# Expert stage of a two-block Flamingo kernel: one row buffer and one result buffer for every tile, eight weight buffers, and an earlier gelu table load

## The chip, the core and the metric

The kernel runs on one core of one Trainium2 chip. The metric is the device time of one execution in microseconds (us); the time given for a kernel is the median of several runs. TensorE is called PE here, VectorE DVE, ScalarE ACT, GpSimd POOL and SyncE SP. An engine executes its own list of instructions in order and waits for others by semaphores. SP and ACT also issue DMAs; a DMA raises a semaphore by 16 when it has landed.

## What is computed

The input is x (4 batches of 256 tokens, 128 features) and a context of 512 rows of 96 features for each batch. Four residual blocks follow one another: single-head cross-attention with softmax, a feed-forward block whose operands are quantized to FP4 and back, 16-head cross-attention with a small feed-forward tail, and a mixture of 8 experts, of which every token takes one. All are preceded by a layer norm and multiplied by a tanh gate. The part that the change touches is the last block:

```python
router_probs = jax.nn.softmax(x @ Wr, axis=-1)
expert_idx = jnp.argmax(router_probs, axis=-1)
p_max = jnp.max(router_probs, axis=-1, keepdims=True)
def expert_mlp(w1, bb1, w2, bb2):                  # 128 -> 512 -> 128
    h = jax.nn.gelu(x @ w1 + bb1, approximate=False)
    return h @ w2 + bb2
outs = jax.vmap(expert_mlp)(W1, b1, W2, b2)        # 8 experts
out = p_max * jnp.einsum('te,etd->td', onehot, outs)
...
x = x + jnp.tanh(g_ffn[1]) * out
```

## The kernel before

Up to about 281 us of the span the kernel works through the first three blocks and the routing, batch by batch, in an order written out by hand (CHAINS, walked by `walk` on every engine). At the end of each batch, POOL scatters that batch's 256 finished rows to `row_dram`, a buffer in DRAM with one region for each expert. Such a row of 260 numbers (PAY) holds the normed input of the expert (128), the residual (128), the gate, and the token's number. Each scatter raises `rows_scattered`.

Then comes the expert stage. 1024 tokens in tiles of 128 rows, where a tile belongs to one expert, are at most 8 + 7 = 15 tiles (TILES). DVE works out a plan from the counts (14 small steps, semaphore `plan_dve`): for each tile its expert and the DRAM row at which it begins, both put into `exp_i`. Unused tiles point to blank rows, whose token number lies out of range, so that nothing is written for them; they go through the same work.

For tile k each engine has one share:

- **SP** (`load_rows`) reads the tile's DRAM row out of `exp_i` into a register (`row_of`, a TENSOR_LOAD and two register steps, L436) and issues the load of 128 rows of 260 numbers from `row_dram` to `xg` (L439).
- **ACT** (`w1_load`, L1157 and L1158) reads the tile's expert in the same way and issues the load of that expert's first matrix (256 KB) to a slot of `w1s`. In `act_tile` it computes four gelus of 128x128 (L1166) and then issues a further `w1_load`.
- **PE** turns the rows (`pe_turn`, one transpose, L895), multiplies by the first matrix (`pe_up`, four products in two halves) and by the second (`pe_down`: a product that adds the bias, then four that each wait for one gelu). The second matrices of all experts stand in SBUF. The order in the loop is turn(k+2), up(k+1), down(k).
- **DVE** copies the turned rows from PSUM (`dve_turned`, L1555) and forms gate times result plus residual into `eo` (`dve_tile`, L1565).
- **POOL** scatters `eo` to the output by token number (L1875), one indirect DMA for each tile.

In the profile the names `xg`, `eo`, `xgT`, `ehT` all appear as `pT`, because these buffers are parts of that tensor, and many PE instructions have the line of a helper (L564).

Buffers go round in rings of RING = 5: `xg`, `eo`, `xgT`, `ehT` and `w1s`. The row load of tile k, from tile 5 on, therefore waits until the scatter of tile k-5 has landed (`out_scattered[k % 5]`, in `load_rows`), because that scatter reads the token numbers out of the same part of `xg`. The weight load of tile k+5 is issued after the gelus of tile k. `load_rows` reads the first five row numbers into registers, then waits for `rows_scattered`, then issues five loads.

Of the kernel before, what the change touches and what calls it, by code (L numbers as in the profile page):

```python
# [5 lines left out]
ALU = mybir.AluOpType  # L6
# [19 lines left out]
RING = 5  # L26
# [139 lines left out]
def flamingo_kernel(nc, a):  # L166
    out = a["out"]
    with ExitStack() as ctx:
# [45 lines left out]
        w1s = sb("w1s", [P, RING * F])  # L214
# [122 lines left out]
        xg = pT[:, 0:RING * PAY]  # L337
        o = RING * (PAY + D)
        xgT = pT[:, o:o + RING * P]
        ehT = pT[:, o + RING * P:o + RING * (P + F)]  # L340
        b1_pick = pT[:, o + RING * (P + F):o + RING * (P + F) + TILES * FC * E]
        eo = pT[:, RING * PAY:RING * (PAY + D)]
# [49 lines left out]
        rows_loaded = [sem(f"rows_loaded{u}") for u in range(RING)]  # L392
        out_scattered = [sem(f"out_scattered{u}") for u in range(RING)]
        e_turned, e_up, e_down = sem("e_turned"), sem("e_up"), sem("e_down")
        e_xT, e_act, e_out = sem("e_xT"), sem("e_act"), sem("e_out")
        w1_slot_loaded = [sem(f"w1_slot_loaded{u}") for u in range(RING)]
# [36 lines left out]
        def load_rows(sp):  # L433
# [4 lines left out]
            def load(k, row):  # L438
                sp.dma_start(xg[:, (k % RING) * PAY:(k % RING + 1) * PAY], row_dram[bass.ds(row, P), :]  # L439
                             ).then_inc(rows_loaded[k % RING], 16)  # L440
# [12 lines left out]
        def _(sp):  # L453
# [105 lines left out]
            for u in range(RING):  # L559
                sp.wait_ge(out_scattered[u], 16 * (TILES // RING))  # L560
# [307 lines left out]
        def slot(x, u, w):  # L868

            u = u % RING  # L870
            return x[:, u * w:(u + 1) * w]
# [18 lines left out]
        def pe_turn(pe, k):  # L890

            pe.wait_ge(rows_loaded[k % RING], 16 * (k // RING) + 16)
# [4 lines left out]
        def pe_up(pe, k):  # L897

            pe.wait_ge(e_xT, k + 1)
            pe.wait_ge(w1_slot_loaded[k % RING], 16 * (k // RING) + 16)  # L900
            if k >= 2:
                pe.wait_ge(e_act, FC * (k - 1))
            for half in range(2):
                for c in (2 * half, 2 * half + 1):
                    last = mm(up_bank(k, c), slot(w1s, k, F)[:, c * P:(c + 1) * P], slot(xgT, k, P))
                last.then_inc(e_up, 1)

        def pe_down(pe, k, e):
# [4 lines left out]
            for c in range(FC):  # L913
                pe.wait_ge(e_act, FC * k + c + 1)
                last = mm(down_bank(k), slot(ehT, k, F)[:, c * P:(c + 1) * P], w2e[:, bass.ds(e * F + c * D, D)], False,
# [984 lines left out]
```

## Time and profile before

| what | value |
|---|---|
| time, median of 3 runs | 345.93 us (345.71 to 347.42) |
| time of the profiled execution | 347.22 us |
| its span, first to last instruction | 345.5 us |
| PE busy | 262.1 us, 76% |
| DVE busy | 196.7 us, 57% |
| ACT busy | 159.7 us, 46% |
| POOL busy | 97.7 us, 28% |
| mean DMA rate | 89 GB/s |

The span is the time from the first to the last instruction of the profiled execution; 1.7 us of its time lie around the span. Busy shares are means over the whole program. The expert stage takes about the last 60 us of it, and what bounds that stage is read from windows, waits and the chain there. The expert tiles are slow or fast with the clock that TensorE was granted, 1.2 or 2.4 GHz, shown as 0.50 or 1.00 in the windows.

### The profile page before, as it was taken

The numbers are of one execution on the slowest core, as the hardware profiler recorded it, in microseconds if no ns is written. First come the engines' busy times: TensorE is split into PE (matmuls) and PEld (weight loads), VectorE is DVE, ScalarE is ACT, GpSimd is POOL, SyncE is SP. The second block draws the span as 40 slices with busy tenths as digits, with TensorE's granted clock in tenths as the row PEclk, the third lists the DMA queues.
The fourth block names the chain that finished last, engine by engine and source line by source line (L and its number), as shares of the span: only waits on it lengthen the run. The fifth ranks groups of instructions, "written<-read, shape, count | busy, mean of one in ns | idle before, by whom it ended". The sixth has DMA issues, their size and how long they took to land.

```text
span 345.5 us, 7087 instructions
## 1 busy us (share of the span) xinstructions
PE 262.1 (76%) x2617; PEld 144.2 (42%) x2617; DVE 196.7 (57%) x509; ACT 159.7 (46%) x371; POOL 97.7 (28%) x224
## 2 busy tenths in 40 slices
PE   3689477586877999979769998989976422968874
PEld 1236134132432435544335453444432212858764
DVE  6953775538993789797895767676521161111211
ACT  2335324453256548675544857366851202323331
POOL 5003314522462213451413412310320120132323
PEclk9999699769996999999988999699987555598999
DMA  4697792830052010232101321030000008254410
GB/s 112 197 264 250 258 308 85 265 108 9 2 161 77 6 37 4 73 100 72 38 1 41 61 82 38 31 73 1 3 33 0 0 15 244 71 150 109 148 42 8
DMA packets 30032, 30.89 MB, mean 89 GB/s; under 512 B 5445, under 2 KB 25116, under 8 KB 29998
## 3 DMA queue, kind: packets, MB, share of 16 engines
q1 hardware_dynamic: 18029, 16.06, 16.8%
q10 hardware_dynamic: 11104, 12.78, 11.7%
q0 software_dynamic: 864, 1.59, 1.4%
q8 instruction: 21, 0.34, 0.4%
q14 instruction: 14, 0.11, 0.1%
HBM read 15.28 MB, written 15.42 MB: 89 GB/s over the span
## 4 chain that ended last, share of the span: by engine, by line
PE 46%; DVE 25%; ACT 8%; DMA 7%; POOL 6%; issue 6%; SPq 1%; POOLq 0%; ACTq 0%; DVEq 0%
PE psC L564 10%; DVE nmx L1454 8%; PE psB L564 7%; PE psA L564 7%; PE psX L569 5%; PE psG L569 5%; PE psD L569 5%; DMA pT<-row_dram 3%; ACT pT L1119 3%; DMA out_rows<-pT 3%; POOL rstd L1669 2%; PE psG L564 1%; PE psD L575 1%; DMA qs<-nmT 1%; DVE stat L1227 1%
## 5 line engine op out<-in xcount | busy, mean ns | idle before, releaser
L1454 DVE TENSOR_REDUCE nmx<-psB 128x1 f32<-128x512 f32 x128 | 82.9, 680 | 28.3 <-PE psB L564 27.5
L1119 ACT ACTIVATE pT<-psA 128x512 f32<-128x512 f32 x128 | 72.0, 599 | 15.2 <-PE psA L564 13.8
L564 PE MATMUL psB<-ks,qs 112*128 112x512 bf16 x128 | 49.8, 402 | 8.5 <-DVE nmx L1454 8.0
L564 PE MATMUL psA<-qs,ks 115*128 115x256 bf16 x256 | 50.2, 282 | 6.2 <-ACT pT L1119 4.2
L564 PE MATMUL psC<-pT,v_live 128*32 128x256 f32 x512 | 37.0, 439 | 0.7 <-ACT pT L1119 0.7
L564 PEld LDWEIGHTS psA<-qs,ks 115*128 115x128 bf16 x256 | 20.2, 99 | 32.3 <-ACT pT L1119 12.9
L1875 POOL DMA_INDIRECT out_rows<-pT x15 | 14.8, 983 | 43.8 <-DVE pT L1565 43.5
L564 PEld LDWEIGHTS psB<-ks,qs 112*128 112x128 bf16 x128 | 12.5, 100 | 29.1 <-DVE nmx L1454 19.9
L564 PEld LDWEIGHTS psC<-pT,v_live 128*32 128x32 f32 x512 | 17.5, 126 | 16.9 <-issue 9.1
L569 PE MATMUL psG<-guT,xqT 128*32 128x352 f32 x128 | 15.1, 551 | 3.5 <-DVE u L1324 3.5
L1051 ACT ACTIVATE p<-psD,nmx 128x512 f32<-128x512 f32 x8 | 5.5, 688 | 26.6 <-DVE nmx L1303 26.6
L1166 ACT ACTIVATE pT<-psA,b_tiles 128x128 f32<-128x128 f32 x32 | 9.4, 367 | 17.1 <-PE psA L564 17.1
L1129 ACT COPY ou<-psC 128x256 f32<-128x256 f32 x16 | 5.9, 367 | 23.8 <-PE psC L564 23.8
L1679 POOL CAST nmp<-nmx 128x8 bf16<-128x8 f32 x16 | 3.1, 192 | 46.9 <-DVE nmx L1454 46.9
L569 PE MATMUL psD<-k0T,q0T 128*32 128x512 f32 x64 | 12.0, 833 | 3.8 <-DVE x_all L1317 3.2
L1819 POOL DMA_INDIRECT row_dram<-pay,desti x8 | 8.3, 1032 | 22.8 <-DVE count L1547 21.6
L1662 POOL TENSOR_TENSOR ve<-mv,eps_t 128x2 f32<-128x2 f32 x16 | 3.2, 199 | 38.7 <-DVE mv L1231 38.7
L1166 ACT ACTIVATE pT<-psB,b_tiles 128x128 f32<-128x128 f32 x28 | 8.1, 368 | 12.9 <-PE psB L564 12.9
L895 PE MATMUL psD<-ident,pT 128*128 128x128 f32 x8 | 2.8, 344 | 14.5 <-DMA pT<-row_dram 14.5
L1689 POOL TENSOR_TENSOR q_norm<-hid,q_inv 128x352 f32<-128x352 f32 x8 | 6.3, 788 | 25.2 <-DVE q_inv L1257 25.2
L1695 POOL TENSOR_TENSOR hid<-q_add,q_scale 128x352 f32<-128x352 f32 x8 | 6.3, 787 | 22.4 <-DVE q_add L1275 22.4
L1565 DVE SCALAR_TENSOR_TENSOR pT<-psC,pT 128x128 f32<-128x128 f32 x8 | 2.8, 351 | 16.8 <-PE psC L564 16.8
(227 smaller groups left out, 492.3 us busy)
## 6 DMA issues: line engine op xcount, KB each, us to landing
row_dram<-ou ACTq DMA_DIRECT2D x13, 650.0 KB, 6.2
w1s<-in_L_ffn_W ACTq DMA_DIRECT2D x15, 256.0 KB, 2.8
ks<-k_parts SPq DMA_DIRECT2D x16, 192.0 KB, 3.2
pT<-row_dram SPq DMA_DIRECT2D x15, 130.0 KB, 2.7
k_parts<-k1p SPq DMA_DIRECT2D x4, 384.0 KB, 3.2
qs<-q_parts SPq DMA_DIRECT2D x16, 96.0 KB, 3.5
k_parts<-k1p SPq DMA_DIRECT2D x4, 256.0 KB, 3.2
ctx_in<-in_ctx SPq DMA_DIRECT2D x4, 192.0 KB, 2.7
```

Source lines behind the costliest of these rows:

```text
L564: return nc.tensor.matmul(o, l, r, start=start, stop=stop, **k)
L569: last = nc.tensor.matmul(o[32 * j:32 * j + 32, :], l[:, 32 * j:32 * j + 32], r, start=start, stop=stop, skip_group_check=True)
L1051: nc.scalar.activation(p0[:, :], psD[:, :], ACT.Exp, bias=nmx0[:, t:t + 1], accum_out=sum0[:, t:t + 1]).then_inc(*aact.step(b, f"p{t}"))
L1119: nc.scalar.activation(pT[:, o:o + 512], psA[:, (i % 2) * 512:(i % 2) * 512 + 512], ACT.Exp).then_inc(*probs.step(b, f"e{g}_{i}"))
L1129: nc.scalar.copy(ou[:, g * LQ:(g + 1) * LQ], psC[:, 0:LQ]).then_inc(*ou_ready.step(b, f"g{g}"))
L1166: nc.scalar.activation(slot(ehT, k, F)[:, c * P:(c + 1) * P], up_bank(k, c), ACT.Gelu, bias=b1_tiles[:, k * FC + c:k * FC + c + 1]).then_i ...
L1454: nc.vector.tensor_reduce(nmx[:, col:col + 1], psB[:, (i % 2) * 512:(i % 2) * 512 + 512], AX_X, ALU.max, negate=True).then_inc(*maxima.ste ...
L1669: nc.gpsimd.tensor_tensor(rstd[:, o:o + NT], ve[:, o:o + NT], neg_half[:, :], ALU.pow).then_inc(*steps.step(b, f"{p}_rs"))
L1689: nc.gpsimd.tensor_tensor(q_norm[:, o:o + n].rearrange("p (n i) -> p n i", i=QB), src.rearrange("p (n i) -> p n i", i=QB), wide(q_inv[:, o ...
L1695: nc.gpsimd.tensor_tensor(dst.rearrange("p (n i) -> p n i", i=QB), q_add[:, o:o + n].rearrange("p (n i) -> p n i", i=QB), wide(q_scale[:, ...
L1819: nc.gpsimd.indirect_dma_start(row_dram[:, :], bass.IndirectOffsetOnAxis(desti[:, t:t + 1].bitcast(U32), 0), pay[:, t * PAY:(t + 1) * PAY] ...
L1875: nc.gpsimd.indirect_dma_start(out, bass.IndirectOffsetOnAxis(token, 0), eo[:, u * D:(u + 1) * D], None, bounds_check=T - 1, oob_is_err=Fa ...
```

## The change

Each of the 15 tiles gets its own part of `xg` and of `eo`. For this, `xgT` goes round in a ring of 3 and `ehT` in a ring of 2, and `b1_pick` moves from `pT` to `q_norm`. `load_rows` no longer waits for scatters: it reads a row number and issues that tile's load, fifteen times over, and waits for `rows_scattered` once, after the first row number. The weights get eight slots (W1_RING); ACT issues eight weight loads ahead of its first gelu, and the load of tile k+8 after the gelus of tile k. The throwaway gelu that makes ACT load the gelu table stands ahead of the wait for the plan and no longer behind the weight loads. DVE's wait for `out_scattered` in `dve_tile` goes, and the five `out_scattered` semaphores become one, which SP waits for at the end.

```diff
-RING = 5
+W1_RING = 8
+XT_RING = 3
+H_RING = 2
...
-        xg = pT[:, 0:RING * PAY]
...
-        eo = pT[:, RING * PAY:RING * (PAY + D)]
+        o = TILES * (PAY + D)
+        xg = pT[:, 0:TILES * PAY]
+        eo = pT[:, TILES * PAY:o]
+        xgT = pT[:, o:o + XT_RING * P]
+        ehT = pT[:, o + XT_RING * P:o + XT_RING * P + H_RING * F]
+        b1_pick = q_norm[:, 0:TILES * FC * E]
...
             sp.wait_ge(plan_dve, PLAN)
-            rows = {k: row_of(k) for k in range(RING)}
-            sp.wait_ge(rows_scattered, 16 * B * NT)
-            for k in range(RING):
-                load(k, rows[k])
-            for k in range(RING, TILES):
+            for k in range(TILES):
                 row = row_of(k)
-                sp.wait_ge(out_scattered[k % RING], 16 * (k // RING))
-                load(k, row)
+                if k == 0:
+                    sp.wait_ge(rows_scattered, 16 * B * NT)
+                sp.dma_start(xg[:, k * PAY:(k + 1) * PAY], row_dram[bass.ds(row, P), :]).then_inc(rows_loaded[k], 16)
...
-            if k + RING < TILES:
-                w1_load(act, k + RING)
+            if k + W1_RING < TILES:
+                w1_load(act, k + W1_RING)
...
+            nc.scalar.activation(th[:, 0:1], gains[:, 0:1], ACT.Gelu)
             act.wait_ge(plan_dve, PLAN)
-            for k in range(RING):
+            for k in range(W1_RING):
                 w1_load(act, k)
-            nc.scalar.activation(th[:, 0:1], gains[:, 0:1], ACT.Gelu)
...
-            if k >= RING:
-                dve.wait_ge(out_scattered[u], 16 * (k // RING))
```

On SP, at the start of the row loads, the order before was as follows. TENSOR_LOAD and "ISA x2" are one `row_of`; the single ISA is the register step of a load. Four more pairs of `row_of` rows stand where the dots are, then four more loads.

```order
L436 TENSOR_LOAD exp_i [waits plan_dve]
L436 ISA x2
...
L439 ISA [waits rows_scattered]
L439 DMA pT<-row_dram 128x260
...
L436 TENSOR_LOAD exp_i
L436 ISA x2
L439 ISA [waits out_scattered0]
L439 DMA pT<-row_dram 128x260
```

The same place with the change:

```order
L438 TENSOR_LOAD exp_i [waits plan_dve]
L438 ISA x2
L445 ISA [waits rows_scattered]
L445 DMA pT<-row_dram 128x260
L438 TENSOR_LOAD exp_i
L438 ISA x2
L445 ISA
L445 DMA pT<-row_dram 128x260
```

One row number instead of five now stands ahead of the first load, one more stands between any two loads, and no load waits for a scatter.

On ACT, between the last activation of the routing (lexp) and the first gelu of the experts, the order before was this, with four more weight loads where the dots are:

```order
L1151 ACTIVATE lexp<-lsub 128x16 [waits tail_dve]
L1157 TENSOR_LOAD exp_i [waits plan_dve]
L1157 ISA x2
L1158 ISA
L1158 DMA w1s<-in_L1_ffn_W1 128x512
...
L1217 ACT_TABLE_LOAD
L1217 ACTIVATE th<-gains 128x1
L1166 ACTIVATE pT<-psA,b1_tiles 128x128 [waits e_up,tile_bias_ready]
```

With the change, and seven more weight loads at the dots:

```order
L1146 ACTIVATE lexp<-lsub 128x16 [waits tail_dve]
L1208 ACT_TABLE_LOAD
L1208 ACTIVATE th<-gains 128x1
L1152 TENSOR_LOAD exp_i [waits plan_dve]
L1152 ISA x2
L1153 ISA
L1153 DMA w1s<-in_L1_ffn_W1 128x512
...
L1161 ACTIVATE pT<-psA,b1_tiles 128x128 [waits e_up,tile_bias_ready]
```

The table load moved ahead of the wait for the plan, and three more weight loads stand ahead of the first gelu.

## Rows read from the trace of the kernel before

**Rows 1.** Waits of PE from 286 us: engine tile line <- releaser: us, times, longest.
```profile
PE psD L895 <- DMA pT<-row_dram: 14.5, 4, 10.6
PE psX L895 <- DMA pT<-row_dram: 3.9, 3, 2.4
```

**Rows 2.** Waits of SP's queue from 280 us, same columns.
```profile
SPq L439 <- DMA out_rows<-pT: 32.2, 8, 11.4
```

**Rows 3.** Chain that ended last: start us, us, what.
```profile
303.10 3.50 DMA out_rows<-pT
306.76 3.00 DMA pT<-row_dram
```

**Rows 4.** PE's timeline: start us, us, line, op, out<-in [idle before <-releaser].
```profile
296.57 2.08 PE L564 MATMUL psC<-w2e,pT 128*128 x8
...
300.71 1.19 PE L564 MATMUL psG<-w2e,pT 128*128 x8
...
303.00 1.16 PE L564 MATMUL psC<-w2e,pT 128*128 x8
...
309.81 0.33 PE L895 MATMUL psD<-ident,pT 128*128 128x128 f32 x1 [2.51 <-DMA pT<-row_dram]
...
311.14 2.08 PE L564 MATMUL psC<-w2e,pT 128*128 x8
...
314.96 1.16 PE L564 MATMUL psG<-w2e,pT 128*128 x8
...
317.21 1.16 PE L564 MATMUL psC<-w2e,pT 128*128 x8
...
336.32 1.16 PE L564 MATMUL psC<-w2e,pT 128*128 x8
```

**Rows 5.** Windows: stretch, us, busy of PE PEld DVE ACT POOL, PEclk, DMA share, GB/s.
```profile
286.00:290.80 4.80, 0.00 (x0) 0.00 (x0) 0.15 (x1) 0.77 (x1) 0.00 (x0) 0.50 0.84 233
290.80:300.50 9.70, 9.13 (x37) 7.87 (x38) 1.34 (x5) 3.85 (x12) 0.66 (x1) 0.50 0.44 144
300.50:310.80 10.30, 7.12 (x55) 6.25 (x54) 1.83 (x6) 3.09 (x11) 3.29 (x4) 0.98 0.50 132
310.80:314.20 3.40, 3.40 (x18) 3.20 (x17) 0.55 (x2) 0.97 (x4) 0.00 (x0) 0.54 0.50 121
314.20:340.00 25.80, 21.25 (x160) 18.49 (x159) 4.92 (x16) 10.37 (x36) 8.84 (x9) 0.99 0.31 87
```

**Rows 6.** Line L436, 284 to 288 us: count, ns min/median/max, first and last start.
```profile
L436 SPq TENSOR_LOAD <-exp_i x5: 266/269/494, 284.5 to 287.0; - x5
...
L436 SPq SEQ_ASSERT  x5: 18/18/33, 285.2 to 287.5; - x5
```

**Rows 7.** Line L1819, the last two scatters to `row_dram`, same columns, then their landing.
```profile
L1819 POOL DMA_INDIRECT row_dram<-pay,desti x2: 963/1002/1042, 282.2 to 283.5; - x2
...
DMA to landing us min/median/max: 2.6/2.7/2.7
```

**Rows 8.** Line L439, the first five row loads, same columns, then their landing.
```profile
L439 SPq DMA_DIRECT2D pT<-row_dram x5: 332/333/398, 287.7 to 289.9; - x5
...
DMA to landing us min/median/max: 3.0/4.4/4.9
```

**Rows 9.** ACT's timeline (ACTq is its queue of DMA issues), columns as in rows 4.
```profile
285.39 4.62 ACTq L1158 DMA_DIRECT2D w1s<-in_L_ffn_W  x5
290.04 1.28 ACT L1217 ACT_TABLE_LOAD   x1 [10.03 <-issue]
...
293.00 0.63 ACT L1166 ACTIVATE pT<-psA,b_tiles 128x128 f32<-128x128 f32 x2 [1.47 <-PE psA L564]
...
316.71 1.14 ACT L1166 ACTIVATE pT<-psB,b_tiles 128x128 f32<-128x128 f32 x4 [1.18 <-PE psB L564]
```

**Rows 10.** POOL's timeline, the last two scatters of results.
```profile
340.80 0.98 POOL L1875 DMA_INDIRECT out_rows<-pT  x1 [1.16 <-DVE pT L1565]
342.08 0.98 POOL L1875 DMA_INDIRECT out_rows<-pT  x1 [0.30 <-issue]
```

More of the change, by code:

```diff
@@ L213, in flamingo_kernel @@
         wr = sb("wr", [P, E])
-        w1s = sb("w1s", [P, RING * F])
+        w1s = sb("w1s", [P, W1_RING * F])
         b1T = sb("b1T", [P, FC * E])
@@ L336, in flamingo_kernel @@
         exp_i = sb("exp_i", [P, 2 * TILES], I32)
-        xg = pT[:, 0:RING * PAY]
[L338 to L341, printed above, removed]
-        eo = pT[:, RING * PAY:RING * (PAY + D)]
+        o = TILES * (PAY + D)
[4 more added lines that the diff above has]
+        b1_pick = q_norm[:, 0:TILES * FC * E]
         tg = sb("tg", [P, 4])
@@ L391, in flamingo_kernel @@
         plan_dve = sem("plan_dve")
-        rows_loaded = [sem(f"rows_loaded{u}") for u in range(RING)]
-        out_scattered = [sem(f"out_scattered{u}") for u in range(RING)]
+        rows_loaded = [sem(f"rows_loaded{k}") for k in range(TILES)]
+        out_scattered = sem("out_scattered")
         e_turned, e_up, e_down = sem("e_turned"), sem("e_up"), sem("e_down")
         e_xT, e_act, e_out = sem("e_xT"), sem("e_act"), sem("e_out")
-        w1_slot_loaded = [sem(f"w1_slot_loaded{u}") for u in range(RING)]
+        w1_slot_loaded = [sem(f"w1_slot_loaded{u}") for u in range(W1_RING)]
         bias_dve2, b1_ready = sem("tile_bias_dve"), sem("tile_bias_ready")
@@ L558, in _ @@
             load_rows(sp)
-            for u in range(RING):
-                sp.wait_ge(out_scattered[u], 16 * (TILES // RING))
+            sp.wait_ge(out_scattered, 16 * TILES)
         def mm(o, l, r, start=True, stop=True, **k):
@@ L866, in pe_steps, with slot @@
             return s
-        def slot(x, u, w):
-            u = u % RING
+        def slot(x, u, w, ring=TILES):
+            u = u % ring
             return x[:, u * w:(u + 1) * w]
@@ L890, in pe_turn @@
         def pe_turn(pe, k):
[L892 removed]
+            pe.wait_ge(rows_loaded[k], 16)
             if k >= 2:
@@ L904, in pe_up @@
                 for c in (2 * half, 2 * half + 1):
-                    last = mm(up_bank(k, c), slot(w1s, k, F)[:, c * P:(c + 1) * P], slot(xgT, k, P))
+                    last = mm(up_bank(k, c), slot(w1s, k, F, W1_RING)[:, c * P:(c + 1) * P],
+                              slot(xgT, k, P, XT_RING))
                 last.then_inc(e_up, 1)
@@ L914, in pe_down @@
                 pe.wait_ge(e_act, FC * k + c + 1)
-                last = mm(down_bank(k), slot(ehT, k, F)[:, c * P:(c + 1) * P], w2e[:, bass.ds(e * F + c * D, D)], False,
+                last = mm(down_bank(k), slot(ehT, k, F, H_RING)[:, c * P:(c + 1) * P], w2e[:, bass.ds(e * F + c * D, D)], False,
                           c == FC - 1)
@@ L1165, in act_tile @@
                     act.wait_ge(e_up, 2 * k + c // 2 + 1)
-                nc.scalar.activation(slot(ehT, k, F)[:, c * P:(c + 1) * P], up_bank(k, c), ACT.Gelu,
+                nc.scalar.activation(slot(ehT, k, F, H_RING)[:, c * P:(c + 1) * P], up_bank(k, c), ACT.Gelu,
                                      bias=b1_tiles[:, k * FC + c:k * FC + c + 1]).then_inc(e_act, 1)
-            if k + RING < TILES:
-                w1_load(act, k + RING)
+            if k + W1_RING < TILES:
+                w1_load(act, k + W1_RING)
         @block.scalar
@@ L1554, in dve_turned @@
             dve.wait_ge(e_turned, k + 1)
-            nc.vector.tensor_copy(slot(xgT, k, P), turn_bank(k)).then_inc(e_xT, 1)
+            nc.vector.tensor_copy(slot(xgT, k, P, XT_RING), turn_bank(k)).then_inc(e_xT, 1)
         def dve_tile(dve, k):
-            u = k % RING
             if k + 2 < TILES:
@@ L1562, in dve_tile @@
             dve.wait_ge(e_down, k + 1)
-            if k >= RING:
-                dve.wait_ge(out_scattered[u], 16 * (k // RING))
-            nc.vector.scalar_tensor_tensor(eo[:, u * D:(u + 1) * D], down_bank(k),
-                                           xg[:, u * PAY + 2 * D:u * PAY + 2 * D + 1],
-                                           xg[:, u * PAY + D:u * PAY + 2 * D], ALU.mult, ALU.add).then_inc(e_out, 1)
+            nc.vector.scalar_tensor_tensor(slot(eo, k, D), down_bank(k), slot(xg, k, PAY)[:, 2 * D:2 * D + 1],
+                                           slot(xg, k, PAY)[:, D:2 * D], ALU.mult, ALU.add).then_inc(e_out, 1)
         @block.vector
```

16 lines of the change are left out of this document (6 added, 10 removed).

## The prediction

> **What bounds the kernel now.** I read the waits of PE in the expert stage first, then the waits of SP's queue, the chain, PE's timeline and the windows. After its first tile PE waits for one thing of weight: row loads. Six waits of 14.5 + 3.9 - 10.6 = 7.8 us in all lie behind the first one of 10.6 us [rows 1]. The row loads in turn waited 32.2 us on SP, 8 times, for scatters of results [rows 2]. So the ring of five closes a loop: scatter of tile k-5, row load of tile k, turn, products, scatter. The chain shows two of its legs, a scatter of 3.50 us from POOL's start to landing and then a row load of 3.00 us [rows 3]. In the first tiles and wherever a row was there in time, PE itself is the bound: 9.13 of 9.70 us busy in the stretch from 290.8 [rows 5].
>
> PE's pace has two values. From the products of one tile (start of the eight that write the result) to those of the next it takes 300.71 - 296.57 = 4.14 us where the clock is 0.50, and 317.21 - 314.96 = 2.25 us where it is 1.00 and no row is awaited [rows 4, 5]. After the wait of 2.51 us that ends at 309.81 the clock falls: the same eight products take 2.08 us at 311.14 and 1.16 us at 314.96 [rows 4], and the stretch 310.8 to 314.2 was granted 0.54, with PE busy for all 3.40 us [rows 5].
>
> **Term 1, the dense stage.** The loop is cut: every row load is issued without a scatter. What is late next is PE. With the products of tile 2 starting at 303.00 and those of tile 12 at 336.32 [rows 4], these ten tiles take 33.3 us now. At 2.25 us each they take 22.5 us: 10.8 us less. That is made up of the 7.8 us of waits [rows 1], about 1.7 us because the 3.4 us stretch at half clock goes [rows 5], and the remaining 1.3 us for the overlap that is lost at each wait, when a transpose can't start under the products ahead of it.
>
> The Trainium skill (TensorE: Matmul & The Clock Gate, section "HAM oscillation — how this bites in real kernels") has the same pattern: a matmul loop that waits for DMA falls back to the low clock and starts its next piece cold, and it names longer uninterrupted work as the cure. By that rule no slow stretch is left in the dense stage. The trace agrees at 309.81 [rows 4], but the other waits, 2.4 us the longest of them on psX [rows 1], fell in a stretch of 0.99 [rows 5]; if the fall at 310.8 was chance and not the wait, the term would be 9.1 us instead.
>
> Do the rows come in time? On SP one row number costs (287.0 - 284.5) / 4 = 0.63 us and one issue (289.9 - 287.7) / 4 = 0.55 us [rows 6, 8]; interleaved, 1.18 us for each tile. The last is issued at 286.4 + 14 x 1.18 = 303 us and lands, by the longest of the first five loads (4.9 us [rows 8]), by 308. From tile 3 on each row is there long before a PE that goes on by 2.25 us or more. POOL can follow: its last two scatters start 1.28 us apart [rows 10]. ACT can follow too: four gelus take 1.14 us [rows 9], and a whole weight load with its TENSOR_LOAD, (4.62 - 0.33) / 4 = 1.07 us from one to the next [rows 9] (0.33 us for the last issue alone, taken from SP's [rows 8]), makes 2.21 us even if nothing of it overlaps.
>
> **Term 2, the start.** This one is not named in the change. Before, SP read five row numbers, from 284.5 to 287.5 [rows 6], and issued its first row load at 287.7 [rows 8]. The last scatter of rows starts at 283.5 and lands 2.7 us later, at 286.2 [rows 7]. So SP, with 0.2 us from its last step to the issue, was late by 1.3 us on its own account. Now only one row number stands ahead, read by about 285.2 [rows 6]; the scatter is the later one, and the load goes out at about 286.4. PE's first turn comes 1.3 us earlier.
>
> It does not all stay. Row 1 is issued at 287.6 and row 2 at 288.8, with 3.0 to 4.9 us to land [rows 8]: row 2 is there between 291.8 and 293.7. PE wants it when it has turned and multiplied tile 0, some 3 us after 289.4 (a first product of 2.08 us at the low clock, as for the second [rows 4], and two transposes and a copy, estimated at 0.3 us each): 292.4. The loss lies between nothing and 1.3 us; I take 0.3, nearer to the low end, since row 2 no longer has rows 3 and 4 behind it within 1.1 us. That leaves 1.0 us of lead at the low clock. If the clock rises at the same moment as before (300.5), the lead is worth 0.5 us; if the rise moves along, 1.0 us. I take 0.8.
>
> **Term 3, edits at nothing.** The eight weight loads: the first is issued at 285.4, each takes 1.07 us, so ACT is free at 285.4 + 7 x 1.07 + 0.33 = 293.2 us, against a first gelu at 293.00 [rows 9]. PE would have its first half product 1.3 us earlier, so the first gelu now waits for ACT's own issues. Its consumer is the second product of tile 0, at about 296.57 - 1.0 = 295.6 [rows 4]; four gelus of 0.63 us a pair [rows 9] end at 294.5. About 1 us of cover is left; without it each further weight load ahead would cost 1.07 us. The table load (1.28 us) lay behind five weight loads and was hidden, as ACT then still waited 1.47 us for PE [rows 9]; where it goes, ACT had idled 10.03 us [rows 9], so it is hidden again. Had it stayed behind eight loads, it would have come to 294.7 and eaten the cover. DVE's wait for a scatter falls away, but the row load of that tile had waited for the same scatter: nothing. The smaller rings of xgT and ehT are written only after PE has passed their last reader in its own order: nothing. The other buffer for b1_pick and the single semaphore at the end change no duration.
>
> **Sum.** 347.22 - 10.8 - 0.8 = 335.6 us against the profiled execution (span 345.5, 1.7 around it). That execution is 1.3 us above the median of the runs, 345.93; against the median the sum is 334.3. With the profiled one, the runs of before lie in two pairs some 1.4 us apart, and a clock that rises or falls once more or less would do that, which would make part of my 1.7 us absent in the faster pair. I take 335.0, between them.
>
> **Rivals.**
> *A: rows 1 and 2 come late.* From 286.4 to 293 SP offers 133 KB each 1.18 us and ACT 262 KB each 1.07 us, 113 + 245 = 358 GB/s, where the DMA engines were 0.84 busy at 233 GB/s from 286.0 to 290.8 [rows 5]; already then loads went from 3.0 to 4.9 us [rows 8]. If row 2 is late by the full 1.3 us or more, the start gains nothing (+0.8), and an idle PE may put off the rise of the clock by as much as the 3.4 us stretch seen at 310.8, at half rate 1.7 us: 337.5. For it speaks that three more weight loads stand in the way; against it that the rows are issued from an emptier queue, 1.3 us earlier. The Trainium skill (DMA: Bandwidth & Descriptors, section "Issuing engines are not separate DMA queues") says that transfers issued by different engines interleave on the same 16 DMA engines; by that rule, loading eight weights ahead takes from the rows, and the time is this rival's.
>
> *B: the clock rises earlier,* since PE starts 1.3 us sooner, by a stretch of up to 3.4 us: 1.7 us more gain, 333.3. For it: the clock was 0.50 for 9.7 us of which PE was busy 9.13 [rows 5], so the rise was near. Against it: it had not come in all that time.
>
> *C: ACT becomes the bound* in the seven tiles that still issue a weight load, if semaphores add 0.3 us to the 2.21 us of term 1: 7 x 0.26 = 1.8 us, 336.8. Against it: 2.25 us was reached at 317.21 with such a load on ACT in between.
>
> *D: slower, the clock stays low.* Place: the dense stage. At 4.14 us instead of 2.25 each tile costs 1.9 us more [rows 4]. The gain of 11.6 is eaten from 11.6 / 1.9 = 6.1 further tiles at the low clock; with all twelve, 358. Against it: where PE worked without long waits, the windows show 0.98 and 0.99 [rows 5], and the change takes waits away.
>
> *E: the rows come no earlier,* because the DMA engines hold them up. For no gain, the row of tile 14, issued at 303, would have to land some 30 us later, where 4.9 us was the longest of five [rows 8]: 346.
>
> **How the numbers follow.** Forecast 0.64 (its own range 333.5 to 336.5), A 0.17, B 0.10, C 0.06, D 0.02, E 0.01. The range runs from below B to above A, 332.5 to 338.2. A measurement of this kernel tells about 0.5% from no change. Faster by over 0.5%: all but D and E, 0.97. Within: 0.01. Slower: 0.02.
>
> **What would show it.** Term 1: no wait of SP's row loads for out_rows, PE's waits for row loads after tile 2 gone, 2.25 us from tile to tile, no slow stretch after the rise. Term 2: the first row load near 286.4 and PE's first turn near 289.4. Term 3: the last of eight weight issues near 292.9, the first gelu right behind, and PE not waiting for it. A: waits of PE for the rows of tiles 1 and 2, and loads above 4 us. What would make me wrong: a low clock beyond 302, a pace above 2.4 us at full clock, or a new wait of PE for ACT.

## The result and the profile after

The changed kernel takes 329.7 us (median; 327.5 to 334.7) against 345.8 us before (344.8 to 347.4): a ratio of 0.956, 95% interval 0.951 to 0.961. The forecast was faster, 335.0 us with a range of 332.5 to 338.2, so the sign was right and the size was not: the kernel came out 5.3 us under the sum. Two later sets of runs of the same two kernels gave 329.5 against 345.3 (ratio 0.953, 0.946 to 0.959) and 331.0 against 343.5 (0.969, 0.957 to 0.980). Single runs of before lie between 338 and 349 us over all sets, which is wider than the three runs that the prediction had seen.

The profiled execution took 328.96 us (span 326.9). First, as in [rows 1] and [rows 2], the waits of PE and of SP's queue from 277 us (engine, tile, line <- releaser: us, times, longest):

```profile
PE psD L889 <- DMA pT<-row_dram: 9.6, 1, 9.6
```
```profile
SPq L445 <- DMA row_dram<-pay,desti: 0.8, 1, 0.8
```

PE waits for the rows of one tile, the first, and no row load waits for a scatter of results any more. What SP waits for now, 0.8 us, is the scatter of rows to DRAM: it comes after the first row number, as term 2 had it. PE's timeline, as in [rows 4] (start us, us):

```profile
285.74 0.47 PE L889 MATMUL psD<-ident,pT 128*128 128x128 f32 x1 [9.64 <-DMA pT<-row_dram]
...
290.89 1.16 PE L558 MATMUL psC<-w2e,pT 128*128 x8
...
293.13 1.16 PE L558 MATMUL psG<-w2e,pT 128*128 x8
...
295.38 1.16 PE L558 MATMUL psC<-w2e,pT 128*128 x8
...
317.86 1.16 PE L558 MATMUL psC<-w2e,pT 128*128 x8
```

From the result of tile 2 (295.38) to that of tile 12 (317.86) there are 22.5 us, 2.25 for each tile; before it was 33.3 us [rows 4]. The windows, as in [rows 5] (stretch, us, busy of PE, PEld, DVE, ACT, POOL, granted clock, DMA share, GB/s):

```profile
281.90:285.70 3.80, 0.00 (x0) 0.00 (x0) 0.17 (x1) 0.00 (x0) 0.00 (x0) 0.50 0.71 215
285.70:290.20 4.50, 3.91 (x16) 3.22 (x17) 0.80 (x3) 0.36 (x2) 0.00 (x0) 0.51 0.99 339
290.20:324.30 34.10, 32.20 (x257) 29.20 (x255) 7.62 (x27) 16.75 (x60) 14.44 (x15) 1.00 0.40 123
```

The clock is at its low level until 290.2, and at 1.00 from there to the last products. PE worked for 4.5 us at the low clock (7.5 and 7.6 us in two later traces of this kernel); before, it was 9.7 us [rows 5]. That is the first thing that the sum did not have.

The second lies ahead of the changed code. The plan's last step on DVE, which writes exp_i, in the trace of before and then in that of after:

```profile
284.25 0.20 DVE L1635 TENSOR_SCALAR exp_i<-t_row 128x15 int32<-128x15 f32 x1
```
```profile
280.18 0.19 DVE L1626 TENSOR_SCALAR exp_i<-t_row 128x15 int32<-128x15 f32 x1
```

4.1 of the 18.6 us between the two spans were there by then. Of the changed instructions only the throwaway gelu on ACT, with its table load, had run, and no step of the plan waits for it. From the last copy of an attention output on ACT (263.64 before, 259.59 after) to the end of the plan it is 20.8 us in both traces, so the 4.1 us lie ahead of that copy. The experiments therefore measure from the end of the plan.

### The profile page after: what moved, and what is told of

It reads as the page before. It is cut to its first block, busy times and chain, and to the rows that moved or that the text cites. A ratio compares the mean times of both kernels' runs of the same rounds, so it can differ in the third digit from the quotient of the medians.

```text
span 326.9 us, 7075 instructions
## 1 busy us (share of the span) xinstructions
PE 252.8 (77%) x2617; PEld 138.1 (42%) x2617; DVE 196.1 (60%) x509; ACT 158.8 (49%) x371; POOL 97.7 (30%) x224
## 3 DMA queue, kind: packets, MB, share of 16 engines
HBM read 15.28 MB, written 15.42 MB: 94 GB/s over the span
## 4 chain that ended last, share of the span: by engine, by line
PE 49%; DVE 26%; ACT 9%; POOL 7%; issue 5%; DMA 3%; POOLq 0%; ACTq 0%; DVEq 0%; SPq 0%
PE psC L558 11%; DVE nmx L1449 8%; PE psB L558 8%; PE psA L558 7%; PE psG L563 5%; PE psX L563 5%; PE psD L563 4%; ACT pT L1114 3%; PE psG L558 3%; POOL rstd L1660 2%; PE psD L569 1%; DMA qs<-nmT 1%; DVE stat L1222 1%; DVE q_add L1266 1%; ACT ln_b L957 1%
## 5 line engine op out<-in xcount | busy, mean ns | idle before, releaser
L558 PE MATMUL psB<-ks,qs 112*128 112x512 bf16 x128 | 49.0, 397 | 8.6 <-DVE nmx L1449 8.2
L558 PE MATMUL psC<-pT,v_live 128*32 128x256 f32 x512 | 35.9, 428 | 0.7 <-ACT pT L1114 0.7
L563 PE MATMUL psD<-k0T,q0T 128*32 128x512 f32 x64 | 11.1, 772 | 3.9 <-DVE x_all L1312 3.2
L1319 DVE SCALAR_TENSOR_TENSOR u<-th,psG 128x352 f32<-128x352 f32 x8 | 4.2, 522 | 14.2 <-ACT th L1057 14.2
L1660 POOL TENSOR_TENSOR rstd<-ve,neg_half 128x2 f32<-128x2 f32 x16 | 11.5, 718 | 0.0
```

Of the source, the lines that this page charges most:

```text
L558: return nc.tensor.matmul(o, l, r, start=start, stop=stop, **k)
L563: last = nc.tensor.matmul(o[32 * j:32 * j + 32, :], l[:, 32 * j:32 * j + 32], r, start=start, stop=stop, skip_group_check=True)
L1660: nc.gpsimd.tensor_tensor(rstd[:, o:o + NT], ve[:, o:o + NT], neg_half[:, :], ALU.pow).then_inc(*steps.step(b, f"{p}_rs"))
```

## The experiments

**Times from the end of the plan.** For every kernel below one execution was traced. The table gives the end of the plan, and counted from it, in us: the issue of the first row load, PE's first turn, the moment from which the windows show the clock at 1.0 in the expert stage, the starts of the results of tiles 2 and 12, and the end of the span; then the median of the times.

| kernel | plan ends | row load | turn | clock up | tile 2 | tile 12 | end | median |
|---|---|---|---|---|---|---|---|---|
| before | 284.45 | 3.26 | 6.37 | 16.4 | 18.55 | 51.87 | 61.0 | 345.8 |
| b_again | 284.44 | 3.27 | 7.00 | 16.4 | 18.97 | 50.82 | 60.0 | 343.6 |
| b_layout | 280.02 | 3.28 | 6.86 | 16.5 | 18.94 | 52.71 | 61.9 | 344.7 |
| weights_only | 281.84 | 3.28 | 7.14 | 16.4 | 19.04 | 48.47 | 57.6 | 341.2 |
| slots_only | 281.57 | 3.26 | 7.14 | 16.4 | 19.04 | 48.74 | 57.9 | 343.1 |
| order_only | 280.43 | 1.75 | 5.38 | 9.7 | 15.00 | 51.58 | 60.7 | 343.4 |
| rows_only | 281.83 | 3.28 | 6.83 | 16.4 | 18.88 | 41.36 | 50.4 | 334.0 |
| after_late | 279.69 | 3.26 | 7.11 | 16.8 | 19.19 | 41.67 | 50.8 | 334.6 |
| ring6 | 284.61 | 2.10 | 5.99 | 13.0 | 16.80 | 40.93 | 50.0 | 334.1 |
| after | 280.37 | 1.81 | 5.36 | 9.7 | 15.01 | 37.49 | 46.6 | 329.7 |
| a_again | 282.58 | 1.79 | 5.39 | 13.0 | 16.50 | 38.98 | 48.1 | 329.5 |
| a_third | 282.50 | 1.81 | 5.54 | 13.0 | 16.59 | 39.07 | 48.1 | 331.0 |
| five_ahead | 280.72 | 1.67 | 3.90 | 13.1 | 16.43 | 38.91 | 48.0 | 328.9 |
| late_table | 278.39 | 1.71 | 5.22 | 10.8 | 15.42 | 37.89 | 47.0 | 329.8 |

**rows_only: the ring alone.** The fifteen buffers and row loads without a wait for scatters; SP's start, five weight slots and the late table load as before. The buffer edits are those of the change; the loop, against the kernel before, is this:

```diff
-            for k in range(RING, TILES):
-                row = row_of(k)
-                sp.wait_ge(out_scattered[k % RING], 16 * (k // RING))
-                load(k, row)
+            for k in range(5, TILES):
+                load(k, row_of(k))
```

> Of the change this has only the row and result buffers for every tile and the row loads without a wait for scatters. The five row numbers ahead of the first load, the ring of five weight slots and the late table load stand as before. My theory (the loop scatter - row load was the bound, term 1): tile 2 to tile 12 takes 22.5 us instead of 33.3, the first turn of PE stays some 6.4 us behind the end of the plan, and the time is 345.8 - 10.8 = 335 us, less up to 2.5 us if the clock rises as early as in the changed kernel. Rival (the larger gain comes from the weights or from the start): a gain under 8 us here, over 338 us.

Measured: 334.0 us (327.9 to 336.9; the traced run took 334.1). PE waits for rows once (same columns as above), then goes through tiles 2 to 12 in 22.5 us (300.72 to 323.19):

```profile
PE psD L893 <- DMA pT<-row_dram: 11.1, 1, 11.1
```
```profile
300.72 1.16 PE L562 MATMUL psC<-w2e,pT 128*128 x8
...
323.19 1.16 PE L562 MATMUL psC<-w2e,pT 128*128 x8
```

The windows of the same kernel show the rise 16.4 us behind the end of the plan (281.83), as in the kernel before, and no fall behind it:

```profile
281.83:298.20 16.37, 8.99 (x37) 7.86 (x37) 2.94 (x9) 4.59 (x12) 0.54 (x2) 0.50 0.75 226
298.20:332.00 33.80, 29.54 (x234) 26.74 (x233) 7.08 (x25) 14.33 (x51) 14.21 (x15) 1.00 0.31 88
```

Term 1 stands: without the loop of scatter and row load these ten tiles take 10.8 us less than in the first trace of before. By the median some 4 us remain to the changed kernel; one untraced run of the four, 327.9 us, is as fast as that kernel, so these four times alone don't show them. after_late, below, does.

**order_only: SP's order alone,** in the kernel before.

```diff
-            rows = {k: row_of(k) for k in range(RING)}
-            sp.wait_ge(rows_scattered, 16 * B * NT)
-            for k in range(RING):
-                load(k, rows[k])
-            for k in range(RING, TILES):
+            for k in range(TILES):
                 row = row_of(k)
-                sp.wait_ge(out_scattered[k % RING], 16 * (k // RING))
+                if k == 0:
+                    sp.wait_ge(rows_scattered, 16 * B * NT)
+                if k >= RING:
+                    sp.wait_ge(out_scattered[k % RING], 16 * (k // RING))
                 load(k, row)
```

> The kernel before with the order of SP alone changed: row number and load in turn, so that one row number instead of five stands ahead of the first row load; ring of five and its waits as before. My theory (term 2): the first row load leaves 1.3 to 1.4 us earlier, measured from the end of the plan, and PE's first turn comes 1.0 to 1.3 us earlier; of that 0.5 to 1.0 us is left at the end, 344.8 to 345.3 us. Rival (the loop of scatter and row load sets the end whenever it starts, or the clock's rise does): no change, 345.8 us, though the first turn is earlier.

Measured: 343.4 us (337.9 to 345.3), beside 345.3 for the kernel before on the same chip; that is below both expectations. In the trace the first row load leaves 1.5 us earlier and PE turns 1.0 to 1.6 us earlier than in the three traces of before, but the clock rises 6.7 us earlier, and the result of tile 2 starts 3.5 us sooner than in the first of them. Behind that, this execution loses it again: tiles 2 to 12 need 36.6 us instead of 31.9 to 33.8. Its windows show the clock falling twice, once after and once in a wait of over 3 us for a row, and its waits behind the first are 8.6 us in all, against 7.8 [rows 1]:

```profile
290.10:300.30 10.20, 6.98 (x56) 6.23 (x55) 1.57 (x6) 3.43 (x12) 2.96 (x3) 1.00 0.49 134
300.30:303.70 3.40, 3.40 (x17) 3.06 (x16) 0.17 (x1) 1.25 (x4) 0.00 (x0) 0.51 0.31 94
303.70:310.60 6.90, 4.62 (x37) 4.05 (x35) 1.44 (x5) 2.29 (x8) 2.95 (x3) 0.99 0.46 131
310.60:317.40 6.80, 5.83 (x26) 5.49 (x27) 0.84 (x3) 1.57 (x6) 0.24 (x1) 0.50 0.33 91
```
```profile
PE psD L894 <- DMA pT<-row_dram: 14.1, 3, 9.7
PE psX L894 <- DMA pT<-row_dram: 4.2, 2, 3.2
```

The span ends 60.7 us behind the plan, as in the kernel before (60.0 to 61.9). In this trace the rival was right (the loop sets the end whenever it starts); one trace, with times that differ by 7 us, does not show it for the kernel. The clock's rise moved further than either theory had it.

How long the loop takes goes with how often the clock falls in it. In the six traces with the old ring, between the results of tiles 2 and 12:

| kernel | falls of the clock | wait for a row at each | longest wait without a fall | tiles 2 to 12 |
|---|---|---|---|---|
| weights_only | 0 | | 1.97 | 29.4 |
| slots_only | 0 | | 2.00 | 29.7 |
| b_again | 1 | 2.60 | 1.33 | 31.9 |
| before | 1 | 2.51 | 2.36 | 33.3 |
| b_layout | 2 | 2.42, 1.84 | 1.11 | 33.8 |
| order_only | 2 | 3.22, 3.25 | 1.19 | 36.6 |

Every fall goes with a wait for a row, but waits of 1.97, 2.00 and 2.36 us passed without one.

**after_late: the same order undone,** in the changed kernel: five row numbers, the wait, then loads.

```diff
-            for k in range(TILES):
-                row = row_of(k)
-                if k == 0:
-                    sp.wait_ge(rows_scattered, 16 * B * NT)
+            def load(k, row):
                 sp.dma_start(xg[:, k * PAY:(k + 1) * PAY], row_dram[bass.ds(row, P), :]).then_inc(rows_loaded[k], 16)
+
+            rows = {k: row_of(k) for k in range(5)}
+            sp.wait_ge(rows_scattered, 16 * B * NT)
+            for k in range(5):
+                load(k, rows[k])
+            for k in range(5, TILES):
+                load(k, row_of(k))
```

> The changed kernel with SP's old order at the start: five row numbers, then the wait for the scatters, then loads; all else as changed. Theory 'the order of SP moves the clock': the first row load is 1.4 to 1.5 us later against the end of the plan, the clock rises 16.4 us behind it instead of 9.7 or 13.0, the third tile's result starts 18.5 to 19 us behind it instead of 15.0 to 16.5, and the kernel takes 2 to 4 us more than the changed one. Rival (only the later start counts, term 2 as predicted): 0.5 to 1.3 us more, with the rise as in the changed kernel.

Beside it on the same chip the changed kernel again:

> The changed kernel a third time, beside the kernels of this set on the same chip: 328 to 332 us, the clock's rise 9.7 or 13.0 us behind the end of the plan, the end of the span 46.5 to 48.1 us behind it.

Measured: 334.6 us (332.4 to 337.0) against 331.0 (327.7 to 334.4), 3.6 us by the medians. By the traces the rise comes 16.8 us behind the end of the plan, against 13.0, and the span ends 2.6 us later; against the first trace of the changed kernel it ends 4.2 us later. The windows of after_late, whose plan ends at 279.69:

```profile
283.00:296.80 13.80, 9.45 (x39) 8.13 (x40) 1.34 (x5) 3.34 (x11) 0.98 (x1) 0.51 0.94 305
296.80:330.00 33.20, 29.10 (x232) 26.47 (x232) 7.07 (x25) 14.08 (x50) 13.76 (x15) 1.00 0.23 62
```

All seven traces with five row numbers ahead have the rise 16.4 to 16.8 us behind the plan, all seven with one (order_only, ring6 and the last five of the table) at 9.7 to 13.1. In the one trace with the ring's loop (order_only) nothing of this was left at the end; without the loop, the order is worth 2.6 to 4.2 us.

**Chance or change: the time ahead of the expert stage.** The changed kernel and the kernel before were traced again, and the kernel before with the weight tile made wider, which puts every later tile where it lies in the changed kernel:

```diff
-        w1s = sb("w1s", [P, RING * F])
+        w1s = sb("w1s", [P, 8 * F])
```

> The changed kernel once more, for a second trace. In its first trace the plan ended at 280.4 us, 4.1 us earlier than in the trace of the kernel before, in code that the change leaves alone, and the clock rose 9.8 us behind the end of the plan, not 16.3. Theory 'chance': both vary from execution to execution; the plan ends anywhere from 280 to 285 us here. Theory 'the change does it' (moved addresses, other program layout): the plan ends again at 280 to 281 us and the clock rises again 9 to 11 us behind it, and the time is 327 to 331 us.

> The kernel before once more, for a second trace of it. Theory 'chance': the end of the plan moves by 1 us or more against the 284.4 us of the first trace (280 to 285 us), and so may the rise of the clock, 16.3 us behind it in the first. Theory 'the change does it': the plan ends again at 284 to 285 us and the clock rises again 15 to 17 us behind it.

> The kernel before with the weight tile made eight slots wide, of which five are used: every SBUF tile behind it lies at the address that it has in the changed kernel, and no instruction is added or moved. Theory 'addresses': the plan ends near 280.4 us and the time falls by some 4 us, to 342 us. Theory 'chance': the same time as before within 1 us, 345 to 347 us, and the end of the plan within the spread of the other traces of the kernel before.

Measured: b_layout takes 344.7 us, a ratio of 1.002 (0.998 to 1.007) to before, and its plan ends at 280.02; that of ring6, with the changed layout, ends at 284.61. The end of the plan varies between 278.4 and 284.6 in the table; the traces of before alone span 280.0 to 284.5, those of the changed kernel 280.4 to 282.6. So nothing shows that the change made the 4.1 us between the two first traces. What does make the end of the plan vary stays open. The clock's rise behind the plan did follow SP's order, as after_late shows: both theories were partly right, each on one of the two questions.

**The weight slots.** With eight slots and the early table load put into the kernel before; with the eight slots alone; and with five slots in the changed kernel (a ring of five in place of eight, and no other edit):

```diff
-W1_RING = 8
+W1_RING = 5
```

> The kernel before with eight weight slots and the gelu table load ahead of the plan, nothing else: rows go through the ring of five as before. My theory (term 3): no change within 1 us, 344.8 to 346.8 us, first gelu 0.2 to 0.4 us later against the end of the plan. Rival (fuller DMA queues hold up the first rows): row loads over 4.5 us, 1 to 2 us slower, 347 to 348 us.

> The kernel before with eight weight slots, and the table load in its old place (behind eight weight loads now instead of five). The first trace of eight slots with the early table load ended 57.6 us behind the end of the plan, against 60.0 to 61.9 of the kernel before, all of it between tile 2 and tile 12. Theory 'weight loads that end earlier leave the loop of scatter and row load undisturbed': again 2 to 4 us faster than before, 341 to 343.5 us. Rival (chance: the loop's pace scatters by several us from trace to trace, 29.4 to 36.6 us so far): 344 to 347 us.

> The changed kernel with five weight slots instead of eight. My theory (eight slots bring nothing, and their issues stand ahead of the first gelu): the first gelu comes 1.5 to 3 us earlier, row 0 lands up to 0.4 us sooner, the time is that of the changed kernel within 0.7 us. Rival (eight slots are needed once the rows are there, since the weight load of tile k+5 would come late): waits of PE on weights and 1 us or more slower.

Measured: five_ahead takes 328.9 us, as the changed kernel. Its first gelu came 6.1 us behind the plan, not 8.9 to 9.5 as in the three traces of the changed kernel. But PE waited 1.5 us for the row of tile 2, the second of two waits of 9.7 us in all, and the clock rose at 13.1, so nothing was left of it:

```profile
PE psD L889 <- DMA pT<-row_dram: 9.7, 2, 8.2
```

In the changed kernel the runs show neither a gain nor a cost of the eight slots. In the old loop they seemed to help: weights_only 341.2 us (ratio 0.983, 0.975 to 0.991), with tiles 2 to 12 in 29.4 us; slots_only 343.1 us with 29.7 us there, but a ratio of 1.005 (0.994 to 1.015). Both traces show a shorter stage, and only one of the two sets of times agrees. These are the two traces of the old ring in which the clock did not fall (the table under order_only); whether weight loads that end earlier bring that about, or chance, stays open.

**late_table: the table load behind the weight loads.**

```diff
-            nc.scalar.activation(th[:, 0:1], gains[:, 0:1], ACT.Gelu)
             act.wait_ge(plan_dve, PLAN)
             for k in range(W1_RING):
                 w1_load(act, k)
+            nc.scalar.activation(th[:, 0:1], gains[:, 0:1], ACT.Gelu)
```

> The changed kernel with the throwaway gelu, and so the table load of 1.3 us and a gelu of 0.2, back behind the eight weight loads. In the changed kernel the first gelu started 9.5 us behind the end of the plan, right after the last weight issue, and the first expert result 10.5 us behind it. My theory (about 1 us of cover was left there, term 3): the first gelu comes 1.3 to 1.7 us later, the first result 0.3 to 1.5 us later, the time 0 to 1.5 us over that of the changed kernel. Rival (the eight issues and the table load are hidden by the slow first products): no change.

Measured: 329.8 us, no change beside 329.5 to 331.0. On ACT the table load stands right ahead of the first gelu, which starts at 288.57, 10.2 us behind the plan:

```profile
279.32 7.82 ACTq L1153 DMA_DIRECT2D w1s<-in_L_ffn_W  x8
287.17 1.28 ACT L1212 ACT_TABLE_LOAD   x1 [13.22 <-issue]
288.46 0.20 ACT L1212 ACTIVATE th<-gains 128x1 f32<-128x1 f32 x1
288.57 0.87 ACT L1161 ACTIVATE pT<-psA,b_tiles 128x128 f32<-128x128 f32 x3
```

That is 0.7 us later than in the first trace of the changed kernel, where the eight issues took 8.43 us instead of 7.82, and 1.2 to 1.3 us later than in its other two, where they took 7.87 and 7.94. The products of the first expert result start 10.9 us behind the plan, within the 10.5 to 11.3 of those three; the cover was enough.

**ring6: a ring of six.**

```diff
+X_RING = 6
...
-        xg = pT[:, 0:TILES * PAY]
+        xg = pT[:, 0:X_RING * PAY]
...
+                if k >= X_RING:
+                    sp.wait_ge(out_scattered[k - X_RING], 16)
...
+            if k >= X_RING:
+                dve.wait_ge(out_scattered[k - X_RING], 16)
```

> The changed kernel with a ring of six row and result buffers instead of fifteen, so that the row load of tile k waits for the scatter of tile k-6. Theory 'loop': from the products of tile k-6 to the turn of tile k there are then four tiles of 2.25 us, 9.0 us, for a result step (0.35), the way to POOL (0.8), a scatter to its landing (2.1 to 3.9) and a row load to its landing (2.1 to 4.9), together 5.4 to 10 us: hardly a wait on PE, the time of the changed kernel plus 0 to 2 us. Rival (the gain came from having all loads issued early, not from the length of the loop): half of the gain or less, over 337 us.

Measured: 334.1 us (329.6 to 336.4). The median lies outside both expectations, but its ratio to before, 0.962 (0.950 to 0.974), is not told apart from the 0.953 to 0.969 of the changed kernel. The trace tells more: tiles 2 to 12 take 24.1 us, so one more buffer brings 9.2 of the 10.8 us. PE's waits for rows behind the first are 0.8 us in all:

```profile
PE psD L893 <- DMA pT<-row_dram: 11.1, 3, 10.3
```

Its span ends 50.0 us behind the plan, 1.9 us later than in the two traces of the changed kernel with the rise at 13.0: 1.6 us of that lie between tiles 2 and 12 and the rest at the start, where the first row load left 0.3 us later. So 'loop' holds by the trace. The 336.4 us of the traced run have another part in the late end of its plan, 284.61.

**Throwaway products.** If PE's work brings the clock, PE can be given some while it waits. warm adds 26 products of 112x128 by 512 columns to the changed kernel, warm_five adds them with five weight slots, and warm_tail has 18 more in the routing steps of the last batch. Their results are overwritten.

```diff
+            def spin(n):
+                for _ in range(n):
+                    mm(psA[:, 0:512], identb[0:FILL, :], ks[0:FILL, 0:512])
+            spin(10)
             pe.wait_ge(ew_loaded, 16)
             pe.wait_ge(b_rows_loaded, 48)
             pe.wait_ge(plan_dve, PLAN)
+            spin(10)
+            pe.wait_ge(w1_slot_loaded[0], 16)
+            spin(6)
```

> The changed kernel with 26 throwaway products of 112x128 by 512 columns on PE while it waits for the plan, the first weights and the first rows (10 behind the routing, 10 behind the plan, 6 behind the first weights); their results go to a PSUM bank that the first tile overwrites. In the traces so far the clock rose 16.4 us behind the end of the plan in all five kernels that read five row numbers first, and 9.7 or 13.0 us behind it in all five that read one. Theory 'work of PE brings the clock': it is 1.0 at the first turn, the third tile's result starts at or before 14.3 us behind the plan instead of 15.0 to 16.5, with the first gelu at 9.4 us (behind eight weight issues) as the new bound, and the kernel gains 0.7 to 2.5 us on the changed one. Rival (the moment of the rise doesn't follow PE's work): rise again at 9.7 or 13.0 us, no gain or 1 us lost.

> As the run with 26 throwaway products, with five weight slots instead of eight, so that the first gelu can start about 3 us earlier. Theory 'work of PE brings the clock': the third tile's result starts 12.5 to 14 us behind the end of the plan; 1.5 to 3.5 us faster than the changed kernel, 326 to 328 us. Rival: as the changed kernel, 329 us or more.

> As the run with five weight slots and 26 throwaway products, and 18 more of them behind the last batch's routing steps on PE (behind the turns, the two layers, the logits), where PE waits for other engines and the clock was 0.5 in the traces. Theory 'work of PE brings the clock': the products of these steps take half as long, 1 to 3 us less up to the end of the plan, 324 to 327 us. Rival (the throwaway products delay the steps behind them on PE's queue by as much as they give): 327 to 330 us.

> The version with 44 throwaway products and five weight slots once more, beside the changed kernel on the same chip. If its gain is real: 325 to 327.5 us, 2 to 4 us under the changed kernel, with the clock at 1.0 through the whole expert stage. If the first four runs were chance: 328 us or more.

warm: 330.3 us, no gain. The clock rose during the products and fell again just as the first tile began, after waits of 0.4 and 1.2 us between the groups; it rose again 9.6 us behind the plan (282.21), as in the changed kernel's first trace:

```profile
277.00:288.30 11.30, 8.52 (x35) 3.12 (x35) 6.19 (x30) 1.70 (x3) 2.00 (x2) 0.80 0.40 123
288.30:291.80 3.50, 3.33 (x14) 2.90 (x15) 0.51 (x2) 0.33 (x2) 0.00 (x0) 0.51 0.98 313
291.80:324.00 32.20, 32.20 (x257) 29.23 (x255) 7.28 (x26) 16.77 (x60) 12.81 (x14) 1.00 0.44 134
```

warm_five had 0.99 over the whole expert stage in its trace, with the result of tile 2 at 14.1 us behind the plan, but times from 325.9 to 334.9 us (median 330.5): no gain that the runs show. warm_tail took 326.4 and, in a second set, 326.6 us (325.1 to 329.5) beside 331.0 for the changed kernel on the same chip. Its ratios to before are 0.946 (0.937 to 0.954) and 0.958 (0.949 to 0.968). The 21 us up to the end of the plan, first in the changed kernel and then in warm_tail, there with the expert stage behind them:

```profile
259.00:280.40 21.40, 8.42 (x79) 4.55 (x71) 7.09 (x37) 4.54 (x10) 3.38 (x7) 0.58 0.02 6
```
```profile
258.00:279.20 21.20, 15.99 (x131) 6.80 (x123) 7.09 (x37) 4.53 (x10) 3.35 (x7) 0.86 0.02 7
279.20:322.00 42.80, 38.21 (x286) 32.41 (x286) 10.10 (x34) 17.10 (x60) 14.47 (x16) 1.00 0.52 155
```

In the routing the real products run faster too. The first transpose of the last attention output and the two products of the feed-forward layer, in the changed kernel, then in warm_tail:

```profile
260.02 0.66 PE L806 MATMUL psX<-ident,ou 128*128 128x128 f32 x4 [0.50 <-ACT ou L1124]
...
263.80 1.93 PE L563 MATMUL psX<-oT,ff_w 128*32 128x256 f32 x16 [0.46 <-ACT oT L1129]
266.70 1.93 PE L563 MATMUL psX<-ff_w,hT 128*32 128x128 f32 x32 [0.96 <-ACT hT L1135]
```
```profile
261.45 0.66 PE L806 MATMUL psX<-ident,ou 128*128 128x128 f32 x4 [0.50 <-ACT ou L1144]
...
265.01 1.07 PE L563 MATMUL psX<-oT,ff_w 128*32 128x256 f32 x16 [0.24 <-ACT oT L1149]
...
267.04 1.08 PE L563 MATMUL psX<-ff_w,hT 128*32 128x128 f32 x32 [0.42 <-ACT hT L1155]
```

From that transpose to the end of the plan it takes 20.4 us in the changed kernel (280.37) and 17.8 in warm_tail (279.21): 2.6 us less. From the end of the plan to the end of the span it takes 45.4 and 45.5 us in the traces of its two sets, against 46.6 to 48.1 in the changed kernel. The version with throwaway products in both places is faster than both kernels; by the medians, 3 to 5 us under the changed one.

## Why the prediction was right or wrong

**Term 1 was right,** to the tenth: tiles 2 to 12 take 22.5 us, the waits for rows and the fall of the clock are gone, and the part that has only this (rows_only) shows it alone. The 33.3 us that it set out from are one trace; the three of before have 33.0 in the mean. The Trainium skill's rule (TensorE: Matmul & The Clock Gate, section "HAM oscillation — how this bites in real kernels") held too: the clock stayed at 1.00 from 290.2 to 324.3 where no wait for a DMA was left.

**Term 2 was right in its mechanism and mis-sized.** SP issued its first row load 1.8 us behind the plan instead of 3.3, and PE turned 1.0 us earlier. The step that failed is "I take 0.8": I let the rise move by the lead of 1.0 us at most, and left an earlier one to rival B, at 1.7 us more and a chance of 0.10. In every trace with the new order the rise came earlier, by 3.3 to 6.7 us, and in those of the changed kernel the result of tile 2 started 2.0 to 3.5 us sooner than in the first trace of before. The paces account for that: at 2.25 us a tile instead of 4.14, an estimate from [rows 4] is 1.6 us for a rise 3.4 us earlier and 3.1 us for one 6.7 us earlier, and 0.5 us for a turn 1.0 us earlier, together 2.1 and 3.6. Term 2 is 2.0 to 3.5 us by the traces, 3.6 us by the medians of after_late and a_third. Why the rise moves by so much more than the turn stays open, and it does not simply follow the turn: five_ahead turned 1.5 us before the changed kernel, and its clock rose at 13.1. The argument against B, that the rise "had not come in all that time", was none: it said nothing of what an earlier first turn would do.

**Term 3 was right in the changed kernel:** five slots, or a late table load, change nothing. The first gelu started right behind ACT's last issue (289.84, with eight issues in 8.43 us from 281.31), and PE was not held:

```profile
281.31 8.43 ACTq L1153 DMA_DIRECT2D w1s<-in_L_ffn_W  x8
289.84 1.14 ACT L1161 ACTIVATE pT<-psA,b_tiles 128x128 f32<-128x128 f32 x4 [12.39 <-issue]
```

**The base was a part of the miss.** The sum was made against 347.2 and 345.9 us; the kernel before lies at 343.5 to 345.8 in the set of the result and those that followed. The mean stage of its three traces (before, b_again, b_layout) ends 61.0 us behind the plan, that of the three of the changed kernel 47.6: 13.4 us, of which 10.5 lie between tiles 2 and 12 and 2.8 ahead of that. The gain by the medians is 12 to 16 us from set to set. So of the 5.3 us between forecast and result, 1.8 us are the stage (13.4 against 11.6: term 2 has 2.0 more, term 1 0.3 less), about 1.5 us the base (346.6, the middle between the two, against some 345.1), and about 2 us belong to no step: plan ends vary by 6 us from trace to trace, and why the times of the result's set lie 16 us apart where the stages differ by 13.4 stays open.

**Rivals.** A did not come in the changed kernel: its first five row loads took 2.8 to 4.4 us to land,

```profile
L445 SPq DMA_DIRECT2D pT<-row_dram x5: 337/338/398, 282.2 to 286.7; - x5
...
DMA to landing us min/median/max: 2.8/3.5/4.4
```

and row 2 was there in time, though the DMA engines were 0.99 busy from 285.7 to 290.2. The rule of the Trainium skill (DMA: Bandwidth & Descriptors, section "Issuing engines are not separate DMA queues") that made this rival is borne out only in that the engines were full; PE paid nothing, except for the 1.5 us in five_ahead. B was the case: in two of the three traces of the changed kernel the rise came earlier by the 3.4 us that B named at most, in the first by 6.7. C, D and E did not come: the pace stayed at 2.25 us with a weight load for each of seven tiles, the clock stayed up, and the rows came early. The range was too narrow below because B's price was capped at one stretch as long as the one at 310.8, and because the spread of the runs was taken from three.

## What to carry to other kernels

Count a ring's slack in time: tiles between the reuse of a buffer and its next need, times the pace that you hope for, against the landing of the store and then of the load; five tiles were too few here, and the sixth brought most of the gain. Look also at what a queue does ahead of its first load: five register reads ahead of a wait that needed one cost 1.4 us on SP and, with the clock's later rise, 2.6 to 4.2 us at the end. A lead at the start of a stage at low clock can be worth more than its length, if the clock comes up earlier with it; here one of 1.0 us was worth 2.0 to 3.5 us, and a further 1.5 us in five_ahead nothing. Price it with the rise where it was, and with an earlier one.

## What was not expected of the hardware

The moment of the clock's rise, counted from the end of the plan, lay in three groups: 16.4 to 16.8 us in all seven traces with five row numbers ahead, 13.0 to 13.1 in four with one, and 9.7 to 10.8 in three with one, though the end of the plan itself varied by 6 us. The same kernel fell into two of them: 9.7 in the first trace of the changed kernel, 13.0 in the others. The first turn lay at 6.4 to 7.1 us with five numbers ahead and at 3.9 to 6.0 with one, and the earliest turn (five_ahead) did not bring the earliest rise. In warm the clock fell to 0.51 for 3.5 us though PE had been busy 8.5 of the 11.3 us ahead.

Issuing a DMA is not always a third of a microsecond: in the first trace of the changed kernel, with loads of both queues in flight, one of ACT's issues took 0.93 us and one of SP's 0.83 us, where the median is 0.36 and 0.34. That was one execution: in the other two traces of that kernel the longest took 0.42 (ACT) and 0.47 us (SP), and in the kernel before none of ACT's took over 0.38. ACT's and SP's issues in that first trace, then ACT's in the kernel before (count, ns min/median/max, first and last start):

```profile
L1153 ACTq DMA_DIRECT2D w1s<-in_L_ffn_W x15: 344/362/925, 281.3 to 302.8; - x15
```
```profile
L445 SPq DMA_DIRECT2D pT<-row_dram x15: 337/338/825, 282.2 to 298.6; - x15
```
```profile
L1158 ACTq DMA_DIRECT2D w1s<-in_L_ffn_W x15: 344/349/378, 285.4 to 324.8; - x15
```
